# A graph network on one core: second layer moved ahead of the gathered rows' turning, results used a round later, eight slots in place of four

## Chip, cores and metric

One Trainium2 chip, one of its cores. The metric is the device time of one execution in microseconds, as the median of several runs; lower is better. The profile is one further execution of the same program.

## What is computed

A table of 12,500 nodes with 16 features and a list of 400,000 edges, sorted by receiver (`dst`), with 8 features each. Cut to what matters:

```
h = relu(layernorm(x));  x = x + degree-normed sum over edges of h[src] at dst
h = relu(layernorm(x))
n = LN(MLP(h));  e = LN(MLP(edge_attr))              # encoders, width 64
for s in 0, 1:
    e = e + LN(MLP_s(concat[e, n[src], n[dst]]))      # edge step
    agg = segment_sum(e, dst)
    n = n + LN(MLP'_s(concat[n, agg]))                # node step
out = x + decoder(n)
```

An MLP is `silu(a @ w0 + b0) @ w1 + b1`, all widths 64.

## The kernel before

Everything is float32 but for some helper products. Edges are worked through in 391 rounds of 1,024 slots. A round is two chunks of 512 edges, stacked on the 128 partitions (64 features each), and each chunk's receivers lie in one window of 64 nodes. After a preparation (lists, degrees) three stages run over all rounds, each an own block of programs for the engines:

- **the first layer** (`first_layer`, names `fl_`): the first sum over edges and the edge encoder. Sender rows of x are gathered by GpSimd into a ring of 64 rounds (`gather_sender_x`, L157), up to 53 rounds ahead of their use;
- **two edge steps** (`edge_step`, names `edge_blk_`). In each round GpSimd gathers 8 x 128 rows of the sender table (`sender_part`, L2053) into one of four buffers `g`, as soon as `pre` of four rounds back is signalled. SyncE loads the receivers' numbers `dlb`, the two windows `win` and the edge state `e` (256 KB), in `operands`, two rounds after its own loop count, and stores the new edge state in `store`. VectorE makes the one-hot matrices `oha` (receivers, for taking rows out of the window) and `ohb` (for summing). TensorE adds three products in one bank `h_ps`: window by one-hot (L2102), edge state by weight (L2104), and the gathered rows turned by the identity (L2107); then signals `pre`. ScalarE applies silu (`h`), TensorE the second layer (`second`, L2088 and L2090, into `y_ps`), ScalarE and VectorE the norm (`scale`, `normed`, giving `t`), TensorE the window sums (`sums`, L2069) and, in the first of the two steps (`keep`), the turning of `t` (`turn`, L2078); VectorE adds the sums to `agg` (`add_sums`, L2195) and makes the new edge state `new` (`finish`, L2203).

The order on each engine is written out by hand in a `body(n)`, with work of earlier rounds as `n.back(k)`. Before, TensorE's body of an edge step is: sums and turn of round n-3, second layer of n-1, then the three products of round n, the last of which waits for the gathers. VectorE's: both one-hots of n, addition and finish of n-3, norm of n-1.

The node steps run inside the stages: `rounds_and_nodes` has a main loop, and a late loop of 12 passes with 16 rounds each, into which the pieces of one node tile (`NodeTiles`, lines 1140 to 1380) are set per pass. The 13th node tile is done whole at the end (`nodes_again`), and its stores must be out before the next stage's gathers start.

`rounds_and_nodes` is where the code's size comes from. `Slot(m, b)` stands for round `m * QUAD + b`. `QUAD` is the number of buffers that the code writes out, and so the number of rounds in one pass of the main loop: with 4, the loop `Fori(2, 49)` has 47 passes of four rounds, with eight rounds written out before it and three after it. Semaphores of transfers also go by `n.b`, one for each of the QUAD slots.

Of the kernel before, what the change touches and what calls it, by code (L numbers as in the profile page):

```python
# [14 lines left out]
P = 128  # L15
# [7 lines left out]
TILES = 4  # L23
# [19 lines left out]
QUAD = 4  # L43
# [54 lines left out]
class Slot:  # L98
# [16 lines left out]
    @property  # L115
    def half(self):
        return self.b % 2

# [1393 lines left out]
def first_layer(nc, idx_all, loc_all, gr, g_in, take_ok, key_d, x_parts, part_f, buf, attr_d, xg_d, edge_d, base_sb, agg, enc_w0, w_mid, b1_parts, one_bf, sum_g, ident, row_f, vecs, eps_c, count_sb, raw, s_at, work):  # L1512

    with ExitStack() as ctx:
# [11 lines left out]
        attr = many(QUAD, "attr", [P, 8, E_DIM])  # L1526
        gx = many(QUAD, "gx", [P, TILES, 2, D + XG])
        t = many(QUAD, "t", [P, TILES, 2, D])
        ohb = many(QUAD, "ohb", [P, 8, WIN])
        e = many(QUAD, "e", [P, CHUNK])  # L1530
# [7 lines left out]
        low_key = many(QUAD, "low_key", [P, P], F16)  # L1538
# [25 lines left out]
        with nc.Block() as block:  # L1564
            @block.sync
            def _(sp):
                def store(n):
                    if n.exists():
                        wait(sp, e_ok, n)
                        sp.dma_start(edge_d[bass.ds(n.n, 1)].rearrange("a p c -> (a p) c"), e[n.b][:, :]).then_inc(e_out[n.b], 16)  # L1570

                def body(n, i=None, j=None):
                    wait(sp, turned_in, n.back(4))
                    sp.dma_start(attr[n.b][:, :, :], attr_v[bass.ds(unsorted + n.n, 1)].rearrange("a p j c -> (a p) j c")).then_inc(attr_in[n.b], 16)
                    wait(sp, hot_ok, n.back(4))
                    sp.dma_start(low_key[n.b][:, :], key_v[bass.ds(n.n, 1), PER, :].broadcast_to([P, P])).then_inc(key_in[n.b], 16)
# [21 lines left out]
            def _(pe):  # L1598
# [22 lines left out]
                def turn_in(n):  # L1621
                    wait(pe, attr_ok, n.back(1))
                    landed(pe, attr_in, n)
                    held(pe, passed)
                    nc.tensor.transpose(at_ps[0:64, 0:P], attr[n.b][:, :, :].rearrange("p j c -> p (j c)"),
                                        ident[:, :]).then_inc(turned_in, 1)

                def sums(n):
# [6 lines left out]
                    for c in range(2):  # L1635
                        to = agg_ps[0:XROW + XG, WIN * c:WIN * c + WIN]
                        for i in range(TILES):
                            ins = nc.tensor.matmul(to, gx[n.b][:, i, c, :], ohb[n.b][:, c * TILES + i, :],  # L1638
                                                   start=i == 0, stop=i == TILES - 1)
# [13 lines left out]
                def turn(n):  # L1653
# [3 lines left out]
                    for i in range(TILES):  # L1657
                        ins = nc.tensor.transpose(t_ps[:, P * i:P * i + P], t[n.b][:, i, :, :].rearrange("p c d -> p (c d)"),
# [37 lines left out]
                last = rounds_and_nodes(pe, body, count_sb, 2)  # L1696
# [14 lines left out]
            def _(act):  # L1711
# [38 lines left out]
                last = rounds_and_nodes(act, body, count_sb, 2)  # L1750
# [12 lines left out]
            def _(dve):  # L1763
# [7 lines left out]
                def one_hots(n):  # L1771
                    if not n.exists():
                        return
                    v.tensor_tensor(ohb[n.b][:, :, :], keys[:, 0:WIN].rearrange("p (j w) -> p j w", j=1).broadcast_to([P, 8, WIN]),  # L1774
# [9 lines left out]
                def scaled(n):  # L1784
# [5 lines left out]
                    for to in (t[n.b][:, :, :, :], gx[n.b][:, :, :, 0:D]):  # L1790
# [4 lines left out]
                def take(n):  # L1795
# [4 lines left out]
                    v.tensor_copy(gx[n.b][:, :, :, D:D + X_DIM].rearrange("p i c d -> p (i c) d")[:, 0:PER, :],  # L1800
# [3 lines left out]
                def hot(n):  # L1804
# [4 lines left out]
                    for c in range(KEYS // P):  # L1809
                        ins = v.tensor_scalar(low_hot[n.half][:, P * c:P * c + P], low_key[n.b][:, :], part4[:, c:c + 1], None, ALU.is_equal)  # L1810
                    ins.then_inc(hot_ok, 1)

                def select(n):
# [7 lines left out]
                    v.tensor_reduce(gx[n.b][:, TILES - 1, 1, D:D + X_DIM], of_top[:, :, :].rearrange("p h d -> p d h"), AX_X,  # L1821
# [15 lines left out]
                def finish(n):  # L1837
# [4 lines left out]
                    v.tensor_scalar(e[n.b][:, :], t_ps[:, :], col("g"), col("beta"), ALU.mult, ALU.add).then_inc(e_ok, 1)  # L1842
# [79 lines left out]
                for b in range(QUAD):  # L1922
# [24 lines left out]
                last = rounds_and_nodes(dve, body, count_sb, 2)  # L1947
# [18 lines left out]
def edge_step(nc, idx_all, loc_all, local_d, edge_d, ps_d, pr_d, base_sb, agg, w_in, w_mid, b1_parts, one_bf, ident, row_f, part64,  # L1966
              vecs, eps_c, mlp, keep, count_sb, work):

    with ExitStack() as ctx:
# [13 lines left out]
        dlb = many(QUAD, "dlb", [P, CHUNK], BF16)  # L1983
        win = many(QUAD, "win", [P, P])
        g = many(QUAD, "g", [P, TILES, P])
        e = many(QUAD, "e", [P, CHUNK])
        new = many(QUAD, "new", [P, CHUNK])
        t = many(QUAD, "t", [P, TILES, 2, D])
        ohb = many(QUAD, "ohb", [P, 8, WIN])
        oha = many(2, "oha", [P, CHUNK])  # L1990
# [3 lines left out]
        idle = sb("idle", [P, 2])  # L1994
# [12 lines left out]
        with nc.Block() as block:  # L2007
            @block.sync
            def _(sp):
                def store(n):  # L2010
                    if keep and n.exists():
                        wait(sp, new_ok, n)
                        sp.dma_start(edge_d[bass.ds(n.n, 1)].rearrange("a p c -> (a p) c"), new[n.b][:, :]).then_inc(e_out[n.b], 16)

                def operands(n):
# [4 lines left out]
                    for c in range(2):  # L2020
                        q = slice(64 * c, 64 * c + 64)
                        sp.dma_start(dlb[n.b][q, :], local_v[bass.ds(n.n, 1), c, :].broadcast_to([64, CHUNK])).then_inc(dlb_in[n.b], 16)
                    for c in range(2):
                        q = slice(64 * c, 64 * c + 64)
                        sp.dma_start(win[n.b][q, q], pr_d[bass.ds(at[c], WIN), :]).then_inc(win_in[n.b], 16)
# [10 lines left out]
                for k in (2, 1):  # L2036
                    operands(last.back(k))
                    store(last.back(k + 4))
                for k in (4, 3, 2, 1):
                    store(last.back(k))  # L2040
                if keep:
                    for k in (4, 3, 2, 1):
# [4 lines left out]
            def _(pool):  # L2047
                def body(n):
                    if n >= QUAD:
                        pool.wait_ge(pre, n - QUAD + 1)  # L2050
                    for j in range(8):
                        c, i = j // TILES, j % TILES
                        pool.indirect_dma_start(  # L2053
                            out=g[n % QUAD][:, i, 64 * c:64 * c + 64], out_offset=None, in_=ps_d,
# [6 lines left out]
            def _(pe):  # L2061
                def sums(n):
# [4 lines left out]
                    for i in range(TILES):  # L2067
                        for c in range(2):
                            ins = nc.tensor.matmul(agg_ps[D * c:D * c + D, 0:WIN], t[n.b][:, i, c, :],  # L2069
                                                   ohb[n.b][:, TILES * c + i, :], start=i == 0, stop=i == TILES - 1)  # L2070
                    ins.then_inc(sum_ok, 1)

                def turn(n):
# [3 lines left out]
                    for i in range(TILES):  # L2077
                        ins = nc.tensor.transpose(t_ps[:, P * i:P * i + P], t[n.b][:, i, :, :].rearrange("p c d -> p (c d)"),  # L2078
# [15 lines left out]
                def body(n, i=None, j=None):  # L2094
# [5 lines left out]
                    landed(pe, win_in, n, 32)  # L2100
                    wait(pe, oha_ok, n)
                    nc.tensor.matmul(h_ps[n.half][:, :], win[n.b][:, :], oha[n.half][:, :], start=True, stop=False)  # L2102
                    landed(pe, e_in, n)
                    nc.tensor.matmul(h_ps[n.half][:, :], w_in[:, :], e[n.b][:, :], start=False, stop=False)  # L2104
                    landed(pe, g_in, n, 128)
                    for i in range(TILES):
                        ins = nc.tensor.matmul(h_ps[n.half][:, P * i:P * i + P], g[n.b][:, i, :], ident[:, :], start=False,  # L2107
# [3 lines left out]
                last = rounds_and_nodes(pe, body, count_sb, 2)  # L2111
                for k in (3, 2, 1):
                    sums(last.back(k))
                    turn(last.back(k))
                    if k == 3:
# [4 lines left out]
            def _(act):  # L2120
                def warm(func):
                    k = 0 if func == ACT.Silu else 1
# [10 lines left out]
                def silu(n, i=None, j=None):  # L2133
                    warm(ACT.Silu)
# [5 lines left out]
                    warm(ACT.Sqrt)  # L2140

                def body(n, i=None, j=None):
                    scale(n.back(1))
# [4 lines left out]
                    silu(n, i, j)  # L2148
                    if i is not None:
                        nodes.act_late_dma(act, i, j)  # L2150

                nodes.act_begin(act)
                last = rounds_and_nodes(act, body, count_sb, 2)
# [8 lines left out]
            def _(dve):  # L2162
                v = nc.vector

                def one_hots(n):
                    landed(dve, dlb_in, n, 32)
                    wait(dve, pre, n.back(2))
                    v.tensor_tensor(oha[n.half][:, :], dlb[n.b][:, :], keys[:, WIN:WIN + 1].broadcast_to([P, CHUNK]),  # L2168
                                    ALU.is_equal).then_inc(oha_ok, 1)
                    v.tensor_tensor(ohb[n.b][:, :, :], keys[:, 0:WIN].rearrange("p (j w) -> p j w", j=1).broadcast_to([P, 8, WIN]),  # L2170
# [3 lines left out]
                def normed(n):  # L2174
# [7 lines left out]
                    v.tensor_tensor(t[n.b][:, :, :, :].rearrange("p i c d -> p (i c) d"), y_ps[n.half][:, :].rearrange("p (k d) -> p k d", d=D),  # L2182
# [15 lines left out]
                def finish(n):  # L2198
# [3 lines left out]
                    landed(dve, e_out, n.back(4))  # L2202
                    v.scalar_tensor_tensor(new[n.b][:, :], t_ps[:, :], col("g"), e[n.b][:, :], ALU.mult, ALU.add).then_inc(new_ok, 1)  # L2203
# [9 lines left out]
                for b in range(QUAD):  # L2213
# [5 lines left out]
                last = rounds_and_nodes(dve, body, count_sb, 2)  # L2219
                add_sums(last.back(3))  # L2220
                finish(last.back(3))
                normed(last.back(1))
                for k in (2, 1):
# [26 lines left out]
```

## Time and profile before

| | |
|---|---|
| median of 3 runs | 11666.72 us (11663.32 to 11670.03) |
| profiled execution, first to last instruction | 11672.6 us |
| first layer, main loop, then late loop | about 719 to 2018, then to 3712 us |
| first edge step, first to last gather | 3769.4 to 7676.2 us |
| second edge step, first to last gather | 7722.6 to 11628.2 us |
| busy share: GpSimd, TensorE, VectorE, ScalarE | 73%, 70%, 53%, 46% |

PE is TensorE's matmuls and PEld its weight loads, DVE is VectorE, ACT is ScalarE, POOL is GpSimd, SP is SyncE; a q behind the name means the engine's instruction queue (register work, branches, issued transfers), which isn't counted as busy. In a row, the name before "<-" is written and those behind it are read. "Idle before" an instruction is put down to what ended it; "issue" means that the engine waited for nothing that the profile shows. Times of places are in us from the first instruction.

### The profile page before, as it was taken

What the parts mean: (1) busy time and instruction counts of PE and PEld (TensorE: products, weight loads), DVE (VectorE), ACT (ScalarE), POOL (GpSimd) and SP (SyncE); (2) the same over time, 40 slices, a digit from 0 to 9 for tenths busy, and PEclk for the clock granted to TensorE, in tenths of its full rate; (3) what the DMA queues carried; (4) which work ended last, traced back from release to release, by engine and by line L of the source; (5) the groups of instructions that cost most, each with busy time, mean ns of one, the idle gap of its engine ahead of it and who ended that gap; (6) DMA issues with size and microseconds to landing.
All of it is one profiled execution on the core that took longest, in us unless ns stands there. A gap on an engine that the chain in (4) does not pass through costs nothing. (4 is left out here: it accounts for less than half of the span.)

```text
span 11672.6 us, 199199 instructions
## 1 busy us (share of the span) xinstructions
PE 8130.9 (70%) x55867; PEld 6189.3 (53%) x55867; DVE 6224.5 (53%) x13945; ACT 5398.6 (46%) x8550; POOL 8560.3 (73%) x9018
## 2 busy tenths in 40 slices
PE   5778888888887666666666666666666666666666
PEld 4667777666665444444455545444444444444444
DVE  9988888777776444444444444433333333333333
ACT  0146666555554444444444444444444444444444
POOL 6777777777772777777777777767777777777776
PEclk8789999999998888888888888878888888888888
DMA  2322222222222333333344434432222223323332
GB/s 75 63 44 53 53 53 54 52 53 53 53 52 50 93 97 95 95 95 95 97 104 103 102 100 102 104 78 70 69 69 69 69 70 72 72 71 73 72 72 58
DMA packets 1363893, 866.26 MB, mean 74 GB/s; under 512 B 896223, under 2 KB 1049840, under 8 KB 1362557
## 3 DMA queue, kind: packets, MB, share of 16 engines
q1 hardware_dynamic: 960162, 583.07, 18.3%
q0 software_dynamic: 287776, 227.99, 12.1%
q10 hardware_dynamic: 115376, 49.25, 1.7%
q14 instruction: 432, 3.54, 0.1%
q8 instruction: 147, 2.41, 0.1%
HBM read 627.59 MB, written 247.78 MB: 75 GB/s over the span
## 5 line engine op out<-in xcount | busy, mean ns | idle before, releaser
L2053 POOL DMA_INDIRECT edge_blk_g<-sender_part,idx_all x6256 | 5909.0, 945 | 2157.3 <-issue 1905.3
L2107 PE MATMUL edge_blk_hps<-ident,edge_blk_g 128*128 128x128 f32 x6256 | 1214.8, 354 | 2724.2 <-DMA edge_blk_g<-sender_part,idx_all 2724.2
L157 POOL DMA_INDIRECT gather_ring<-sender_x,idx_all x2422 | 2291.4, 946 | 775.9 <-issue 771.4
L2107 PEld LDWEIGHTS edge_blk_hps<-ident,edge_blk_g 128*128 128x128 f32 x6256 | 1021.2, 247 | 3373.2 <-DMA edge_blk_g<-sender_part,idx_all 3371.9
L2195 DVE SCALAR_TENSOR_TENSOR agg<-edge_blk_aggps,vecs,agg 64x64 f32 x1564 | 442.6, 283 | 3198.3 <-PE edge_blk_aggps L2069 3034.3
L2123 ACT ACT_TABLE_LOAD x1564 | 2006.6, 1283 | 60.2 <-ACTq L1151 32.0
L2137 ACT ACTIVATE edge_blk_h<-edge_blk_hps,vecs 128x512 f32<-128x512 f32 x782 | 537.5, 687 | 2972.2 <-PE edge_blk_hps L2107 2962.5
L2090 PEld LDWEIGHTS edge_blk_yps<-w_edge_blk,edge_blk_h 128*128 128x128 f32 x6256 | 1141.7, 255 | 65.0
L2178 DVE TENSOR_REDUCE edge_blk_red<-edge_blk_sq 128x8 f32<-128x512 f32 x782 | 536.2, 686 | 1157.0 <-ACT edge_blk_sq L2129 1134.0
L2090 PE MATMUL edge_blk_yps<-w_edge_blk,edge_blk_h 128*128 128x128 f32 x6256 | 1100.0, 335 | 0.0
L1714 ACT ACT_TABLE_LOAD x782 | 1003.3, 1283 | 33.2 <-PEq L95 19.0
L1638 PE MATMUL fl_aggps<-fl_ohb,fl_gx 128*96 128x64 f32 x6256 | 666.7, 264 | 452.8 <-DVE fl_ohb L1774 451.0
L1649 PE MATMUL fl_xps<-sender_x_parts,n_was 128*128 128x400 bf16 x4692 | 910.5, 347 | 3.2 <-DVE fl_ohb L1774 3.2
L1638 PEld LDWEIGHTS fl_aggps<-fl_ohb,fl_gx 128*96 128x96 f32 x6256 | 612.8, 177 | 538.6 <-DVE fl_ohb L1774 430.4
L2102 PE MATMUL edge_blk_hps<-edge_blk_oha,edge_blk_win 128*128 128x512 f32 x1564 | 851.3, 627 | 27.9 <-DMA edge_blk_win<-receiver_part 14.4
L1720 ACT ACTIVATE fl_sq<-fl_yps 128x512 f32<-128x512 f32 x391 | 233.3, 597 | 1244.5 <-PE fl_yps L1607 1142.5
L2104 PE MATMUL edge_blk_hps<-edge_blk_e,ew 128*128 128x512 f32 x1564 | 802.0, 594 | 0.0
L2069 PE MATMUL edge_blk_aggps<-edge_blk_ohb,edge_blk_t 128*64 128x64 f32 x12512 | 766.2, 290 | 7.6 <-DVE agg L2195 7.6
L2129 ACT ACTIVATE edge_blk_sq<-edge_blk_yps 128x512 f32<-128x512 f32 x782 | 465.1, 595 | 621.8 <-PE edge_blk_yps L2090 596.6
L2069 PEld LDWEIGHTS edge_blk_aggps<-edge_blk_ohb,edge_blk_t 128*64 128x64 f32 x12512 | 629.9, 193 | 147.1 <-issue 106.1
L1649 PEld LDWEIGHTS fl_xps<-sender_x_parts,n_was 128*128 128x128 bf16 x4692 | 479.7, 102 | 324.0 <-issue 55.7
L2168 DVE TENSOR_TENSOR edge_blk_oha<-edge_blk_dlb,edge_blk_keys 128x512 f32<-128x512 bf16 x782 | 529.4, 677 | 76.7 <-issue 57.9
(284 smaller groups left out, 12163.1 us busy)
## 6 DMA issues: line engine op xcount, KB each, us to landing
edge_blk_e<-edge_state SPq DMA_DIRECT2D x782, 256.0 KB
edge_state<-fl_e SPq DMA_DIRECT2D x391, 256.0 KB
edge_blk_g<-sender_part,idx_all POOLq DMA_INDIRECT x6256
edge_blk_dlb<-local_dst SPq DMA_DIRECT2D x1564, 64.0 KB
edge_state<-edge_blk_new SPq DMA_DIRECT2D x391, 256.0 KB
gather_ring<-sender_x,idx_all POOLq DMA_INDIRECT x2422
edge_blk_win<-receiver_part SPq DMA_DIRECT2D x1564, 16.0 KB
fl_attr<-attr_slots SPq DMA_DIRECT2D x391, 32.0 KB
```

Source lines behind the costliest of these rows:

```text
L157: pool.indirect_dma_start(out=gr[:, n % RING, ring_place(j), :], out_offset=None, in_=table, in_offset=bass.IndirectOffsetOnAxis(ap=idx_al ...
L1638: ins = nc.tensor.matmul(to, gx[n.b][:, i, c, :], ohb[n.b][:, c * TILES + i, :], start=i == 0, stop=i == TILES - 1)
L1649: ins = nc.tensor.matmul(x_ps[:, 0:TOPS * X_DIM], low_hot[n.half][:, P * c:P * c + P], x_parts[:, k, c, :], start=c == 0 and k == 0, stop= ...
L1714: nc.scalar.activation(idle[:, k:k + 1], eps_c[:, :], func)
L2053: pool.indirect_dma_start(out=g[n % QUAD][:, i, 64 * c:64 * c + 64], out_offset=None, in_=ps_d, in_offset=bass.IndirectOffsetOnAxis(ap=idx ...
L2069: ins = nc.tensor.matmul(agg_ps[D * c:D * c + D, 0:WIN], t[n.b][:, i, c, :], ohb[n.b][:, TILES * c + i, :], start=i == 0, stop=i == TILES - 1)
L2090: ins = nc.tensor.matmul(y[:, P * i:P * i + P], h[n.half][:, P * i:P * i + P], w_mid[:, :], start=False, stop=i == TILES - 1)
L2102: nc.tensor.matmul(h_ps[n.half][:, :], win[n.b][:, :], oha[n.half][:, :], start=True, stop=False)
L2104: nc.tensor.matmul(h_ps[n.half][:, :], w_in[:, :], e[n.b][:, :], start=False, stop=False)
L2107: ins = nc.tensor.matmul(h_ps[n.half][:, P * i:P * i + P], g[n.b][:, i, :], ident[:, :], start=False, stop=i == TILES - 1)
L2123: nc.scalar.activation(idle[:, k:k + 1], eps_c[:, :], func)
L2137: nc.scalar.activation(h[n.half][:, :], h_ps[n.half][:, :], ACT.Silu, bias=col("b0")).then_inc(h_ok, 1)
```

## The change

- `QUAD` goes from 4 to 8, and a new constant `BUFS = 4` with a property `buf` takes its place for nearly all buffers, which stay four. So the main loops have eight rounds in a pass, and there are eight transfer semaphores of each kind; `rounds_and_nodes` is called with one written-out pass instead of two.
- In the edge steps `e` has eight buffers, `new` is gone (the new edge state is written over `e`), `oha` has four buffers instead of two.
- TensorE's body: the products of window and edge state of round n, the second layer of n-1, the gathered rows of n, then sums and turn of n-4.
- VectorE's body: `receivers` (oha) of n, addition of n-5, `ohb` of n-1, finish of n-5, norm of n-2. ScalarE's: silu of n first, then the norm's part of n-1.
- SyncE stores eight rounds back, and loads `e` once the store of eight rounds back has landed.

The diff, cut:

```diff
-QUAD = 4
+QUAD = 8
+BUFS = 4
...
+    @property
+    def buf(self):
+        return self.b % BUFS
...
# first layer: all buffers n.b -> n.buf, and on every engine
-                last = rounds_and_nodes(sp, body, count_sb, 2)
+                last = rounds_and_nodes(sp, body, count_sb)
...
# edge step
-        new = many(QUAD, "new", [P, CHUNK])
-        oha = many(2, "oha", [P, CHUNK])
+        oha = many(BUFS, "oha", [P, CHUNK])
...
                     if keep:
-                        wait(sp, new_ok, n.back(4))
+                        landed(sp, e_out, n.back(QUAD))
+                    else:
+                        wait(sp, pre, n.back(QUAD))
                     sp.dma_start(e[n.b][:, :], edge_d[bass.ds(n.n, 1)]...).then_inc(e_in[n.b], 16)

                 def body(n, i=None, j=None):
                     operands(n.back(2))
-                    store(n.back(6))
+                    store(n.back(8))
...
+                def first(n):
+                    landed(pe, win_in, n, 32)
+                    wait(pe, oha_ok, n)
+                    nc.tensor.matmul(h_ps[n.half][:, :], win[n.buf][:, :], oha[n.buf][:, :], start=True, stop=False)
+                    landed(pe, e_in, n)
+                    nc.tensor.matmul(h_ps[n.half][:, :], w_in[:, :], e[n.b][:, :], start=False, stop=False)
+                    second(n.back(1))
+                    landed(pe, g_in, n, 128)
+                    for i in range(TILES):
+                        ins = nc.tensor.matmul(h_ps[n.half][:, P * i:P * i + P], g[n.buf][:, i, :], ident[:, :], ...)
+                    ins.then_inc(pre, 1)
+
                 def body(n, i=None, j=None):
-                    sums(n.back(3))
-                    turn(n.back(3))
-                    second(n.back(1))
+                    first(n)
+                    sums(n.back(4))
+                    turn(n.back(4))
                     if i is not None:
                         nodes.pe_late(pe, i, j)
-                    (the three products of n)
...
                 def body(n, i=None, j=None):          # ScalarE
-                    scale(n.back(1))
+                    silu(n, i, j)
                     if i is not None:
                         ...
-                    silu(n, i, j)
+                    scale(n.back(1))
...
                 def body(n, i=None, j=None):          # VectorE
-                    one_hots(n)
-                    add_sums(n.back(3))
-                    finish(n.back(3))
-                    normed(n.back(1))
+                    receivers(n)
+                    add_sums(n.back(5))
+                    one_hots(n.back(1))
+                    finish(n.back(5))
+                    normed(n.back(2))
...
                 last = rounds_and_nodes(dve, body, count_sb)
+                add_sums(last.back(5))
+                one_hots(last.back(1))
+                finish(last.back(5))
+                normed(last.back(2))
+                add_sums(last.back(4))
+                finish(last.back(4))
                 normed(last.back(1))
-                for k in (2, 1):
+                for k in (3, 2, 1):
                     add_sums(last.back(k))
                     finish(last.back(k))
```

## Rows read from the trace of the kernel before

**Rows 1.** The page, part 1: busy us, share, instructions.
```profile
PE 8130.9 (70%) x55867; PEld 6189.3 (53%) x55867; DVE 6224.5 (53%) x13945; ACT 5398.6 (46%) x8550; POOL 8560.3 (73%) x9018
```

**Rows 2.** GpSimd's waits over the span: us in total, times, longest.
```profile
POOL edge_blk_g L2053 <- issue: 1905.3, 6254, 0.3
...
POOL edge_blk_g L2053 <- POOLq L95: 252.0, 2, 206.6
```

**Rows 3.** Gathers of the first edge step: ns min/median/max, first and last start.
```profile
L2053 POOL DMA_INDIRECT edge_blk_g<-sender_part,idx_all x3128: 940/945/1353, 3769.4 to 7676.2; - x196
```

**Rows 4.** Waits between 4500 and 7500 us, as in rows 2.
```profile
PEld edge_blk_hps L2107 <- DMA edge_blk_g<-sender_part,idx_all: 1234.6, 301, 6.7
```

**Rows 5.** Stretches (main loop; late loops): PE, PEld, DVE, ACT, POOL busy (x count).
```profile
1509.70:1792.10 282.40, 245.98 (x2001) 202.98 (x2000) 250.55 (x641) 173.49 (x280) 213.53 (x227) 1.00 0.29 53
2315.10:3569.40 1254.30, 1046.27 (x7659) 844.28 (x7659) 984.91 (x2493) 647.25 (x1062) 943.64 (x999) 0.92 0.28 52
...
10028.30:11468.10 1439.80, 926.07 (x5661) 657.30 (x5661) 524.66 (x1099) 673.19 (x1054) 1088.81 (x1153) 0.84 0.31 72
```

**Rows 6.** VectorE's waits in ten main passes, 1509.7 to 1792.1 us.
```profile
DVE agg L1835 <- PE fl_aggps L1638: 23.6, 40, 0.8
```

**Rows 7.** The first edge step's end: start, us, engine, instruction.
```profile
7680.60 2.08 PE L2107 MATMUL edge_blk_hps<-ident,edge_blk_g 128*128 128x128 f32 x8 [6.62 <-DMA edge_blk_g<-sender_part,idx_all]
...
7684.64 1.05 PE L2090 MATMUL edge_blk_yps<-w_edge_blk,edge_blk_h 128*128 128x128 f32 x8
...
7687.65 0.69 DVE L2182 TENSOR_TENSOR edge_blk_t<-edge_blk_yps,edge_blk_rs 128x512 f32<-128x512 f32 x1
7689.72 0.70 DVE L2195 SCALAR_TENSOR_TENSOR agg<-edge_blk_aggps,vecs,agg 64x64 f32 x2 [1.38 <-issue]
...
7690.57 0.73 PE L2069 MATMUL edge_blk_aggps<-edge_blk_ohb,edge_blk_t 128*64 128x64 f32 x16 [3.67 <-DVE agg L2195]
...
7691.89 0.70 DVE L2195 SCALAR_TENSOR_TENSOR agg<-edge_blk_aggps,vecs,agg 64x64 f32 x2 [0.68 <-PE edge_blk_aggps L2069]
```

**Rows 8.** VectorE's main-loop branches, first layer: ns, first and last start.
```profile
L171 DVEq COMPARE_BRANCH  x47: 50/56/86, 718.8 to 2018.1; - x47
...
L171 DVEq COMPARE_BRANCH  x1: 56/56/56, 1509.7 to 1509.7; - x1
```

**Rows 9.** VectorE in order of time, main loop and late loop.
```profile
1505.42 0.67 DVE L1774 TENSOR_TENSOR fl_ohb<-fl_aggps,loc_all 128x512 f32<-128x512 f32 x1
...
1510.21 0.68 DVE L1791 TENSOR_TENSOR fl_gx<-fl_yps,fl_rs 128x512 f32<-128x512 f32 x1
...
1512.41 0.67 DVE L1774 TENSOR_TENSOR fl_ohb<-fl_aggps,loc_all 128x512 f32<-128x512 f32 x1
...
3014.89 0.69 DVE L1365 COPY n_stage<-fl_nps 128x512 f32<-128x512 f32 x1 [0.43 <-PE fl_nps L1268]
3018.89 0.63 DVE L1817 SCALAR_TENSOR_TENSOR fl_of_top<-row_f,n_hd,fl_xps 128x400 f32<-128x400 f32 x1 [3.31 <-issue]
```

**Rows 10.** One late-loop branch of VectorE and the record after it.
```profile
L176 DVEq COMPARE_BRANCH  x1: 63/63/63, 3015.0 to 3015.0; - x1
L176 DVEq FUSED_REGOPS  x1: 198/198/198, 3018.5 to 3018.5; - x1
```

**Rows 11.** ScalarE's in the same loop: first and last starts.
```profile
L176 ACTq COMPARE_BRANCH  x9: 45/45/56, 2319.9 to 3436.5; - x9
L176 ACTq FUSED_REGOPS  x9: 128/128/128, 2320.1 to 3436.8; - x9
```

**Rows 12.** VectorE's waits by issue, late loops of first layer, second step.
```profile
DVE fl_of_top L1817 <- issue: 29.7, 9, 3.7
...
DVE edge_blk_oha L2168 <- issue: 22.6, 9, 2.6
```

**Rows 13.** Instruction transfers, main loop (1021.5:1999.5), late loop (2315:3569): packets, MB.
```profile
q14 instruction: 6, 0.05, 0.0%
...
q14 instruction: 74, 0.61, 0.2%
```

More of the change, by code:

```diff
@@ L1695, in _ @@
                 pe.wait_ge(prepared, 1)
-                last = rounds_and_nodes(pe, body, count_sb, 2)
+                last = rounds_and_nodes(pe, body, count_sb)
                 second(last.back(2))
@@ L1749, in _ @@
                 nodes.act_begin(act)
-                last = rounds_and_nodes(act, body, count_sb, 2)
+                last = rounds_and_nodes(act, body, count_sb)
                 square(last.back(2))
@@ L1921, in _ @@
                     step(v.memset(a[:, :], 0.0))
-                for b in range(QUAD):
+                for b in range(BUFS):
                     step(v.memset(gx[b][:, :, :, D + X_DIM:], 0.0))
@@ L1946, in _ @@
                 nodes.dve_begin(dve)
-                last = rounds_and_nodes(dve, body, count_sb, 2)
+                last = rounds_and_nodes(dve, body, count_sb)
                 for k in (2, 1):
@@ L1993, in edge_step @@
         red, sd, rs = (sb(k, [P, 8]) for k in ("red", "sd", "rs"))
-        idle = sb("idle", [P, 2])
+        idle = sb("idle", [P, 2 * QUAD])
         h_ps = [ps(f"hps{i}") for i in range(2)]
@@ L2037, in _ @@
                     operands(last.back(k))
-                    store(last.back(k + 4))
-                for k in (4, 3, 2, 1):
+                    store(last.back(k + 6))
+                for k in (6, 5, 4, 3, 2, 1):
                     store(last.back(k))
                 if keep:
-                    for k in (4, 3, 2, 1):
+                    for k in range(QUAD, 0, -1):
                         landed(sp, e_out, last.back(k))
@@ L2048, in body @@
                 def body(n):
-                    if n >= QUAD:
-                        pool.wait_ge(pre, n - QUAD + 1)
+                    if n >= BUFS:
+                        pool.wait_ge(pre, n - BUFS + 1)
                     for j in range(8):
@@ L2092, in second @@
                     ins.then_inc(y_ok, 1)
+                def first(n):
[7 more added lines that the diff above has]
+                    for i in range(TILES):
+                        ins = nc.tensor.matmul(h_ps[n.half][:, P * i:P * i + P], g[n.buf][:, i, :], ident[:, :], start=False,
+                                               stop=i == TILES - 1)
+                    ins.then_inc(pre, 1)
                 def body(n, i=None, j=None):
-                    sums(n.back(3))
-                    turn(n.back(3))
-                    second(n.back(1))
+                    first(n)
+                    sums(n.back(4))
+                    turn(n.back(4))
                     if i is not None:
                         nodes.pe_late(pe, i, j)
[L2100 to L2107, printed above, removed]
-                                               stop=i == TILES - 1)
-                    ins.then_inc(pre, 1)
-                last = rounds_and_nodes(pe, body, count_sb, 2)
-                for k in (3, 2, 1):
+                last = rounds_and_nodes(pe, body, count_sb)
+                for k in (4, 3, 2, 1):
                     sums(last.back(k))
                     turn(last.back(k))
-                    if k == 3:
+                    if k == 4:
                         second(last.back(1))
@@ L2163, in _, with receivers @@
                 v = nc.vector
-                def one_hots(n):
[L2166 to L2170, printed above, removed]
+                def receivers(n):
+                    landed(dve, dlb_in, n, 32)
+                    wait(dve, pre, n.back(4))
+                    v.tensor_tensor(oha[n.buf][:, :], dlb[n.buf][:, :], keys[:, WIN:WIN + 1].broadcast_to([P, CHUNK]),
+                                    ALU.is_equal).then_inc(oha_ok, 1)
+                def one_hots(n):
+                    if not n.exists():
+                        return
+                    v.tensor_tensor(ohb[n.buf][:, :, :], keys[:, 0:WIN].rearrange("p (j w) -> p j w", j=1).broadcast_to([P, 8, WIN]),
                                     loc_all[:, bass.ds(n.n * 8, 8)].rearrange("p (j w) -> p j w", w=1).broadcast_to([P, 8, WIN]),
@@ L2218, in _ @@
                 nodes.dve_begin(dve)
-                last = rounds_and_nodes(dve, body, count_sb, 2)
-                add_sums(last.back(3))
-                finish(last.back(3))
+                last = rounds_and_nodes(dve, body, count_sb)
+                add_sums(last.back(5))
[4 more added lines that the diff above has]
+                finish(last.back(4))
                 normed(last.back(1))
-                for k in (2, 1):
+                for k in (3, 2, 1):
                     add_sums(last.back(k))
```

78 lines of the change are left out of this document (38 added, 40 removed).

## Prediction

> **What bounds the kernel now.** I read the page first. GpSimd has the most busy time [rows 1]; an average says little here, so I asked what it waits for. Its list is short [rows 2]: the 6,256 gathers of the two edge steps are preceded by "issue" (0.30 us each, its own pace), and only twice, for 252.0 us together, does it wait for a barrier. One edge step's 3,128 gathers start from 3769.4 to 7676.2 [rows 3]: 3906.8 / 3127 = 1.249 us each, 9.99 us for the eight of a round, without a gap. TensorE meanwhile waits for the landing of the gathers, 1234.6 us in 301 rounds [rows 4], 4.1 us a round. So both edge steps run at GpSimd's pace, and TensorE, VectorE and ScalarE have room in every round.
>
> The first layer is different. GpSimd is through with the ring gathers 206.6 us before its first edge gather (the longest wait of [rows 2]), at 3769.4 - 206.6 = 3562.8. In the main loop VectorE is busy 250.55 of 282.40 us [rows 5], and most of what it is idle is the wait for the window sums, 23.6 us in 40 rounds [rows 6], a round trip VectorE starts itself. There the order of work on VectorE sets the round. A microsecond lost by VectorE in the first layer moves the start of the edge steps, and so the end, by a microsecond.
>
> **The order change in the edge steps.** Each instruction of `second`, `sums`, `turn`, `silu`, `scale`, `receivers` and `one_hots` remains, once per round. Moving `second(n-1)` ahead of the gathers' landing lets TensorE do it inside the 4.1 us wait; the wait for the gathers only gets shorter. Value: 0 in steady state, since 9.99 us of GpSimd cover it. Without this cover the gain would be at most the 4.1 us per round that TensorE waits. Results are used a round later, so four receivers' one-hots instead of two are held, and stores go out two rounds later; `new` is gone and `e` has eight buffers. The load of `e` now waits for a store eight rounds back, over 70 us old. GpSimd waits for `pre` four rounds back as before, and that is three rounds ahead of need. Queued behind the new waits on SyncE are the loads of a round two ahead; they were two rounds early and stay so. So 0 for the 782 edge rounds; what would break it is rival 2.
>
> **The ends of the edge steps.** After the last gather nothing hides latency. Before [rows 7]: gathers used at 7680.60, `second` at 7684.64, `t` at 7687.65, an addition at 7689.72, the last sums at 7690.57, the last addition at 7691.89, and then the last node tile. After, TensorE has one more round's sums and turn ahead of `second` (with the additions between them about 2 us), and one more round of additions follows the last `t`: the step from addition to addition is 2.2 us (7689.72 to 7691.89). Finishing one more round's state costs VectorE some tenths. I take +5 us for the first step, +4 us for the second, which has no turning: +9, bounds +3 and +15.
>
> **The loops.** `QUAD` is also the unroll factor of `rounds_and_nodes`. The rounds are the same 391 per stage, but the main loop goes from 47 passes of four rounds to 23 of eight. On the first layer's VectorE a pass takes (2018.1 - 718.8) / 46 = 28.25 us [rows 8]; a round inside one takes 6.99 us (1505.42 to 1512.41, [rows 9]), so the return costs 28.25 - 4 x 6.99 = 0.28 us. Before: 46 x 0.28 = 12.9 us.
>
> What does a return cost when the body has eight rounds? The late loops, with 16 rounds in a pass, show that size matters. On VectorE in the first layer the late branch is at 3015.0 and its next record at 3018.5 [rows 10]; ScalarE in the same loop goes on after 0.2 us (2319.9 to 2320.1, [rows 11]). The time is paid as VectorE idle before its next operation: 29.7 us at 9 returns, and in the second edge step 22.6 us at 9 [rows 12]. Beside it stand instruction transfers: in 978 us of main loop 6 packets on q14 (GpSimd's own straight code), in nine passes of the late loop 74 of 0.61 MB, so 8 per pass of 8.2 KB [rows 13]. A body that is too long is fetched again in each pass, and the engine stands while its top arrives.
>
> How long is too long? I counted every record of an engine between two of its branches, register, wait and load records too (the views' counts leave these out). VectorE: 149 in a main pass of the first layer, 612, 377 and 345 in the late ones: the first goes on at once, the other three stall. SyncE: 377 and 413 stall, 154 doesn't. ScalarE: 168 to 179 don't. TensorE: 1,825 stalls, 1,454 doesn't. By operations alone the new pass has 128 (641 in ten passes, doubled), the late pass of the second edge step 1099 / 9 = 122 and stalls [rows 5]. In records it is 2 x 149 less the second loop control, about 290: between 179 and 345, so the trace doesn't decide it by size. It does by place. The times of the transfers fit a grid of 128 records per packet, each block fetched when the one before it is entered. On this grid the late bodies that stall touch four blocks, those that don't at most three. The main loop starts some 95 records into a block; the earlier `scale` waits for eight semaphores instead of four and adds about 6. 101 + 290 = 391, past 384, the end of the third block: it touches a fourth, by 7 records. I take it that VectorE stalls in each return. SyncE (88), ScalarE (78) and TensorE (866) stay below sizes that don't stall. In the edge steps' main loops VectorE has 186 and SyncE up to 220 records; a stall there of some 3 us per 80 us would lie under GpSimd.
>
> Price: 22 returns. The idle time in the late loop is 29.7 / 9 = 3.3 us; at that branch VectorE had 0.6 us of work left (to 3015.58), in the main loop it has 1.2 (from 1509.7 to 1510.89) [rows 8, 9], so 2.7 us. Low: 22.6 / 9 = 2.5 less half a microsecond, 2.0. High: 2.7 plus another 2, if the fourth block's transfer, which starts just before the return, is still in the way. Sum: 22 x 2.7 - 12.9 = +46.5 us, bounds +31 and +91. The ring gathers aren't in the way (GpSimd is 206.6 us ahead), so nothing hides it.
>
> The Trainium skill (Runtime: NRT & Kernel Launch, "Instruction fetch mechanics") gives an instruction memory of 512 instructions for most engines. By it the new body would fit and this sum be 22 x 0.28 - 12.9 = -6.7 us. The trace speaks against reading it as a loop that may be 512 long, since bodies of 345 and 377 records stall; its remark that a taken branch outside the current window forces a fetch is what rows 10 show.
>
> **Sum.** +46.5 (loops) + 9 (ends) + 0 (rounds) = +55.5 us. On the profiled execution (11672.6 us) that is 11728; on the median of the runs, 11666.72, it is 11722.
>
> **The rivals.**
> 1. No stall: the eight-round body stays in VectorE's instruction memory. By my grid it is 7 records from doing so, and no body between 179 and 345 records has been seen. 22 x 0.28 - 12.9 + 9 = +2 us: 11669, no measurable change. This is the one on the other side; what decides is whether the loop ends before the third block does. Chance 0.16. (The 512 instructions of the Trainium skill's page on the runtime, above, would give this case.)
> 2. Node tiles in the edge steps' late rounds hold VectorE and TensorE so long that GpSimd waits for `pre`. For it: TensorE now does the node work at the end of a round and next wants a one-hot that VectorE makes after its own node work. Against it: GpSimd has three rounds, some 25 us, before it waits, and none of its 6,254 issue gaps is over 0.3 us [rows 2]. Price 2 us for each of 24 tiles: +48, with the stall 11770. Chance 0.05.
> 3. The order change pays: a shorter edge round. It needs GpSimd to issue faster than 1.249 us; nothing in the change touches that, and TensorE's wait shows the room is unused already. 0.1 us for each of 782 rounds would be -78, with the stall 11644. Chance 0.03.
>
> **How the numbers follow.** My forecast has 0.76. Its own range: 22 x 2.0 - 12.9 + 3 = +34 to 91 + 15 = +106, so 11701 to 11773. The range to hold 8 in 10 reaches down to the no-stall case and gives up the top of the forecast's own range, which needs both high bounds: 11664 to 11765. A change within 0.2%, 23 us, can't be told from none in this kernel. Slower: 0.76 + 0.05 and less 0.01 for small stalls = 0.80; same: 0.16; faster: 0.04.
>
> **What would show it.** Right: VectorE idle for 2 to 3 us by "issue" before `select` (the L1817 of before) once per eight rounds in the first layer's main loop; q14 packets in it up from 6 by about four or five per pass of 57 us; GpSimd's barrier wait after the ring gathers longer by some 46 us; gathers of the edge steps still 1.249 us apart; 5 us more between the last gather of a step and what follows. Wrong: few q14 packets in the main loop (rival 1), gaps between GpSimd's edge gathers (rival 2), or less than 3,907 us from first to last gather of a step (rival 3).

## The result, and the profile after

The changed kernel takes 11775.31 us (median of 4 runs, 11770.53 to 11778.12), the kernel before, measured beside it, 11666.53 (11663.32 to 11670.03). The ratio is 1.0094, 95% interval 1.0079 to 1.0108: 108.8 us slower, about twice the 55.5 us forecast and above the range, which ended at 11765. The profiled execution has a span of 11773.7 us, for 11672.6 before.

GpSimd's waits (line, what it waited for; us in total, times, longest):

```profile
POOL edge_blk_g L2059 <- issue: 1906.1, 6254, 0.3
POOL gather_ring L162 <- issue: 867.4, 2724, 37.4
POOL edge_blk_g L2059 <- POOLq L96: 351.9, 2, 299.9
```

Against [rows 2] the gathers' own pace is the same to 0.8 us in 1,906, and the barrier wait between the ring gathers and the first edge gather grew from 206.6 to 299.9 us. So the first edge gather starts 91.6 us later (3861.0 for 3769.4), and nothing was lost inside the edge steps: the first one's gathers

```profile
L2059 POOL DMA_INDIRECT edge_blk_g<-sender_part,idx_all x3128: 940/944/1341, 3861.0 to 7765.3; - x196
```

are (7765.3 - 3861.0) / 3127 = 1.249 us apart, as in [rows 3].

VectorE's waits in the same stretch of the main loop as in [rows 13], 1021.5 to 1999.5 us, the windows of that stretch and of one return of the loop (columns as in [rows 5], PEclk being TensorE's granted clock), the instruction transfers of the stretch, and the branches of the loop:

```profile
DVE agg L1840 <- PE fl_aggps L1643: 89.4, 128, 1.9
DVE fl_of_top L1822 <- issue: 41.2, 16, 2.9
DVE fl_of_top L1822 <- PE fl_xps L1654: 18.6, 16, 1.2
```
```profile
1021.50:1999.50 978.00, 833.42 (x6373) 679.54 (x6373) 801.01 (x2039) 554.44 (x893) 739.33 (x784) 0.94 0.27 50
1180.00:1184.00 4.00, 1.99 (x13) 2.02 (x13) 2.98 (x9) 1.93 (x4) 3.08 (x4) 0.70 0.07 8
1184.00:1188.00 4.00, 4.00 (x17) 2.59 (x17) 2.80 (x7) 0.00 (x0) 2.99 (x4) 0.50 0.21 52
1188.00:1192.00 4.00, 3.62 (x27) 2.90 (x26) 2.81 (x9) 1.60 (x2) 2.87 (x4) 0.94 0.34 45
```
```profile
q14 instruction: 86, 0.70, 0.2%
```
```profile
L176 DVEq COMPARE_BRANCH  x23: 61/69/86, 746.3 to 2097.3; - x23
```

A pass takes (2097.3 - 746.3) / 22 = 61.41 us for eight rounds. Two passes before took 56.5 [rows 8]. The forecast stall is there, once per pass: `select` (L1822, VectorE's operation that reads `fl_xps`) comes 41.2 / 16 = 2.58 us late by "issue", and q14 carries 86 packets instead of 6. But that is only half of what a pass lost. The timeline of one return, VectorE and then TensorE:

```profile
1176.21 0.68 DVE L1796 TENSOR_TENSOR fl_gx<-fl_yps,fl_rs 128x512 f32<-128x512 f32 x1
1179.50 0.63 DVE L1822 SCALAR_TENSOR_TENSOR fl_of_top<-row_f,n_hd,fl_xps 128x400 f32<-128x400 f32 x1 [2.60 <-issue]
...
1181.10 0.67 DVE L1779 TENSOR_TENSOR fl_ohb<-fl_aggps,loc_all 128x512 f32<-128x512 f32 x1
...
1184.94 0.28 DVE L1840 SCALAR_TENSOR_TENSOR agg<-fl_aggps,sum_g,agg 96x64 f32 x1 [1.93 <-PE fl_aggps L1643]
...
1189.27 0.63 DVE L1822 SCALAR_TENSOR_TENSOR fl_of_top<-row_f,n_hd,fl_xps 128x400 f32<-128x400 f32 x1 [1.16 <-PE fl_xps L1654]
```
```profile
1172.15 1.57 PE L1643 MATMUL fl_aggps<-fl_ohb,fl_gx 128*96 128x64 f32 x16 [0.84 <-DVE fl_ohb L1779]
...
1174.01 2.19 PE L1654 MATMUL fl_xps<-sender_x_parts,n_was 128*128 128x400 bf16 x12
...
1182.01 2.79 PE L1643 MATMUL fl_aggps<-fl_ohb,fl_gx 128*96 128x64 f32 x16 [3.69 <-DVE fl_ohb L1779]
1184.59 1.06 PE L1663 MATMUL fl_tps<-ident,fl_t 128*128 128x128 f32 x4
1185.45 3.68 PE L1654 MATMUL fl_xps<-sender_x_parts,n_was 128*128 128x400 bf16 x12
```

While VectorE stands, TensorE runs out of work: it is idle 3.69 us ahead of the window sums, where 0.84 is usual. Behind this idle time the granted clock is 0.50 in the window from 1184 on, the lower of its two levels (1.2 GHz). The sums take 2.79 us instead of 1.57 and the twelve products of `look` (L1654, which make `fl_xps`) 3.68 instead of 2.19, and VectorE waits for both (1.93 us, usually 0.53, and 1.16 us, usually none). Over the 22 returns the interval from one-hot (L1779) to one-hot averages 9.66 and 9.76 us in the two rounds behind the return and 7.00 in the six others. A return that isn't fetched makes the second of the two 7.15 us (seen below, with 28 memsets). That is 2.7 us for the stall and 2.6 us for the slow clock after it. In the trace's record of the granted clock, the main loop has 22 stretches at 0.50, one for each return.

The tally, profile against profile, from the one-hots and the gathers: the main loop (one-hot of round 7 to that of round 199) 1356.0 to 1463.3 us, +107.3; the late loop (to the last one-hot) 1663.2 to 1648.5, -14.7; from the last gather of the first step to the first of the second 46.4 to 53.0, +6.6; behind the last gather of all 44.4 to 50.7, +6.3. Their sum is +105.5. The spans differ by 101.1: the two stretches of gathers are 2.5 and 0.8 us shorter, and 1.0 us is missing ahead of them. The profiled execution of the kernel before is longer than each of its timed runs (11672.6 us against 11663.32 to 11670.03), and that of the changed kernel isn't (11773.7), so the profiles show a few us less than the 108.8 us between the medians.

### The profile page after: what moved, and what is told of

Same layout as the page of the kernel before. It is cut to its first block and busy times, and to the rows that moved or that the text cites. A ratio compares the mean times of both kernels' runs of the same rounds, so it can differ in the third digit from the quotient of the medians.

```text
span 11773.7 us, 196982 instructions
## 1 busy us (share of the span) xinstructions
PE 8245.8 (70%) x55867; PEld 6134.1 (52%) x55867; DVE 6237.5 (53%) x13945; ACT 5328.8 (45%) x8550; POOL 8554.8 (73%) x9018
## 5 line engine op out<-in xcount | busy, mean ns | idle before, releaser
L2103 PE MATMUL edge_blk_hps<-edge_blk_oha,edge_blk_win 128*128 128x512 f32 x1564 | 1168.1, 838 | 278.5 <-DVE edge_blk_oha L2176 273.8
L2096 PEld LDWEIGHTS edge_blk_yps<-w_edge_blk,edge_blk_h 128*128 128x128 f32 x6256 | 859.8, 199 | 315.7 <-issue 290.1
L1654 PE MATMUL fl_xps<-sender_x_parts,n_was 128*128 128x400 bf16 x4692 | 940.1, 354 | 3.2 <-DVE fl_ohb L1779 3.2
L2105 PE MATMUL edge_blk_hps<-edge_blk_e,ew 128*128 128x512 f32 x1564 | 925.3, 677 | 0.0
L2096 PE MATMUL edge_blk_yps<-w_edge_blk,edge_blk_h 128*128 128x128 f32 x6256 | 853.5, 281 | 0.0
L2140 ACT ACTIVATE edge_blk_sd<-edge_blk_red,eps_c 128x8 f32<-128x8 f32 x782 | 234.9, 300 | 989.7 <-DVE edge_blk_red L2190 965.6
L2105 PEld LDWEIGHTS edge_blk_hps<-edge_blk_e,ew 128*128 128x128 f32 x1564 | 383.8, 245 | 560.8 <-issue 559.0
L1654 PEld LDWEIGHTS fl_xps<-sender_x_parts,n_was 128*128 128x128 bf16 x4692 | 490.6, 105 | 344.8 <-issue 87.6
```

What stands on the lines that cost most here:

```text
L1654: ins = nc.tensor.matmul(x_ps[:, 0:TOPS * X_DIM], low_hot[n.half][:, P * c:P * c + P], x_parts[:, k, c, :], start=c == 0 and k == 0, stop= ...
L2096: ins = nc.tensor.matmul(y[:, P * i:P * i + P], h[n.half][:, P * i:P * i + P], w_mid[:, :], start=False, stop=i == TILES - 1)
L2103: nc.tensor.matmul(h_ps[n.half][:, :], win[n.buf][:, :], oha[n.buf][:, :], start=True, stop=False)
```

## The experiments

**Moving the body in instruction memory.** The edit puts k one-column memsets on VectorE ahead of the first layer. They write a tile that nobody reads, once:

```diff
+        shift = sb("shift", [P, 28])
...
                 v.memset(zero_col[:, :], 0.0).then_inc(zero_ok, 1)
+                for k in range(28):
+                    v.memset(shift[:, k:k + 1], 0.0)
```

With 16 of them:

> The changed kernel with 16 more tiny memsets in VectorE's program, in the preparation where VectorE is waiting. Theory (place): on the grid of 128 records the first layer's main loop on VectorE then runs from 118 to 407, still four blocks, so it is fetched again in each return: 11775 us like the changed kernel, within 8. Rival (size): a body of 289 records stalls wherever it lies: 11775 too. Rival (any other layout helps): about 11660. This run is the control for the next one.

Measured: 11773.58 us (11771.51 to 11779.01), ratio to before 1.0095 [1.0078, 1.0112]. (The kernel before took 11663.53 us beside the runs with 16 and 28 memsets, `busy_pe` and `loops_alone`, and 11666.50 beside the other four.) The stretch has 87 q14 packets.

With 28:

> The same with 28 memsets, 12 more than the control. Theory (place): the loop then starts 2 records into a block and ends at 291, three blocks. No stall: the main loop takes 22 x 0.3 us for its returns instead of 22 x 5.4, so 112 us less than the changed kernel: 11663, between 11655 and 11672. Instruction packets of the main loop fall to GpSimd's. Rival (size): 11775, as before.

Measured: 11660.85 us (11649.75 to 11669.84), ratio 0.9998 [0.9988, 1.0008]. Twelve more memsets take 113 us away. The same stretch of the main loop, window and instruction transfers, and the branches:

```profile
1021.50:1999.50 978.00, 857.15 (x6965) 706.80 (x6965) 873.54 (x2232) 604.68 (x977) 739.65 (x783) 1.00 0.29 53
```
```profile
q14 instruction: 7, 0.06, 0.0%
```
```profile
L176 DVEq COMPARE_BRANCH  x23: 50/56/86, 746.4 to 1981.5; - x23
```

The clock is 1.00, the transfers are gone, and a pass takes 56.14 us. Operations, waits and order are those of the changed kernel; only the body's place differs. So each return of the changed kernel costs 61.41 - 56.14 = 5.27 us more than a return that isn't fetched.

**The edge of the block, from the other side.** The same edit with 112 and with 124 memsets:

> The changed kernel with 112 memsets. By the grid the main body (289 records) starts 86 records into a block and ends at 375, inside the third block by 9. Theory of blocks: no stall, main loop about 1347 us as with 28 memsets, clock 1.00; the late body of the first layer spans six blocks (116 + 607 = 723). Time: 11661 if the late loop doesn't care, 11676 if six blocks cost it 15 us. Rival: 28 records helped by another thing than the number of blocks (how far ahead of the branch the last boundary lies, for example): main loop about 1463 us, 11775.

> The changed kernel with 124 memsets, 12 more than the one beside it. The main body starts at 98 and ends at 387, three records inside the fourth block. Theory of blocks: it stalls like the changed kernel itself, main loop 1463 us, clock down to 0.5 behind each stall, some 86 packets on q14 in the window, 11775. Rival: three records in a fourth block cost nothing, or the grid's origin is off by more than two records: 11661.

Measured: 11668.97 us (11660.62 to 11679.6) with 112, 1.0002 [0.9993, 1.0011]; 11785.23 (11780.02 to 11787.02) with 124, 1.0101 [1.0085, 1.0116]. The main loop takes 1350.6 and 1452.5 us, the late loop 1661.1 and 1667.9. Again twelve memsets decide, in the other direction: with 112 nine q14 packets in the stretch and a clock of 1.00, with 124

```profile
1021.50:1999.50 978.00, 833.99 (x6442) 681.08 (x6441) 810.57 (x2061) 560.95 (x903) 739.54 (x783) 0.95 0.27 51
```
```profile
q14 instruction: 87, 0.71, 0.2%
```

By the grid, give or take a record or two, the body reaches 23 records into a fourth block with 16 memsets and 3 with 124; with 28 it lies in three, and with 112 it ends 9 records short of the fourth. So 28 memsets didn't help by a place of their own, since 112 do too. The four runs leave one other reading open: that what counts is how few records lie between the last boundary and the branch (3 to 23 where the body is fetched again, 35 and 119 where it isn't). The late loops speak against it: by the same count the changed kernel's late body of the second edge step ends some 58 records behind a boundary, the late body of the first layer some 99, and both stall.

**Keeping TensorE at work.** In the changed kernel, TensorE multiplies 28 times into the node tile's bank in each pass, at the round where the stall falls; nobody reads the result, and one wait was added ahead of the loop, until VectorE has read what the bank held:

```diff
+                    if n.b == 0 and i is None and not isinstance(n.m, int):
+                        for _ in range(28):
+                            nc.tensor.matmul(n_ps[:, 0:2 * P], one_bf[:, :], b1_parts[:, 0:2 * P], start=True, stop=True)
...
+                        if n.n == 7:
+                            pe.wait_ge(rows_read, 1)
```

> The changed kernel, and in the first round after each return of the first layer's main loop TensorE does 28 products more (96x256, bf16, about 3 us, results unused) while it would wait for VectorE. VectorE's stall of 2.6 us per return stays. Theory (clock): the second half of the loss, 2.7 us per return, is TensorE's granted clock at 0.50 after the idle time; with work in between it stays at 1.00, the sums take 1.57 us again instead of 2.79, and the time falls by 22 x 2.7 = 59 us to 11716 (11705 to 11735; part of it lost if 3 us don't cover the wait). Rival (the second half is a second fetch or VectorE's own order): 11775 or more, since the products come on top.

Measured: 11731.78 us (11729.98 to 11735.96), 1.0058 [1.0041, 1.0075], 43.5 us less than the changed kernel. VectorE's waits and the window of the stretch, and the round behind the stall on TensorE:

```profile
DVE agg L1846 <- PE fl_aggps L1644: 77.5, 132, 1.1
DVE fl_of_top L1828 <- issue: 43.7, 17, 2.6
```
```profile
1021.50:1999.50 978.00, 864.66 (x7078) 715.30 (x7079) 829.45 (x2117) 577.19 (x929) 739.62 (x783) 1.00 0.28 52
```
```profile
1167.53 3.22 PE L1674 MATMUL fl_nps<-b_parts,one_bf 96*128 96x256 bf16 x28
1171.33 1.54 PE L1644 MATMUL fl_aggps<-fl_ohb,fl_gx 128*96 128x64 f32 x16 [0.58 <-DVE fl_ohb L1785]
...
1173.15 2.19 PE L1655 MATMUL fl_xps<-sender_x_parts,n_was 128*128 128x400 bf16 x12
```

The stall stays (43.7 / 17 = 2.57 us) and the clock stays up: sums 1.54 us, `look` 2.19. The two long rounds are now 9.66 and 7.51 us, and the main loop has no stretch at the lower clock. The second half of the price was the clock. A pass takes 59.1 us, so a return still costs 3.0: 2.7 for the stall and 0.4 left in the second round, whose cause I didn't trace. The extra work costs 4.6 us once at the start (the one-hot of round 7 at 704.6 for 700.0) and 1.8 us in the last pass. These and the 0.4 us of each return make up most of the 15.5 us by which the saving falls short of 59.

**The loops without the new order.** The kernel before with eight rounds in a pass and the old edge steps:

```diff
-QUAD = 4
+QUAD = 8
+BUFS = 4
...
-                last = rounds_and_nodes(dve, body, count_sb, 2)
+                last = rounds_and_nodes(dve, body, count_sb)
```

> The kernel before with QUAD = 8 and BUFS = 4 alone: loops of eight rounds, but the old order in the edge steps, the new edge state in its own four buffers. Theory: the whole loss of the first layer is there (91.6 us at the start of the edge steps in the profile), the ends of the edge steps are as before (46.4 and 44.4 us after the last gather instead of 53.0 and 50.7): 13 us less than the changed kernel, 11762 (11752 to 11770). Rival (the order change costs the time): near 11667. Rival (the order change saves time in the steady rounds): over 11775.

Measured: 11760.58 us (11760.29 to 11761.83), 1.0083 [1.0066, 1.01]. The main loop takes 1463.2 us, as after the whole change; behind the two steps' last gathers it is 46.5 and 44.8 us, as before. The new order thus costs 14.7 us between the medians, 12.4 of them seen in these two places, and gives nothing back.

**The loops, moved.** The same kernel with the 28 memsets:

> The eight-round loops alone, with the old order in the edge steps, and 28 one-column memsets on VectorE ahead of the first layer (they write a tile nobody reads). My theory: the loss of the loops is all in the first layer's main loop, because its body touches a fourth block of 128 records. With 28 records more it lies in three. So 11760.58 less what 28 memsets took away from the changed kernel (11773.58 - 11660.85 = 112.7): 11648, which is 0.16% faster than before, since the ends of the edge steps are those of before. In the profile: some 1347 us for the main loop's rounds (round 7 to 199), about 7 packets on q14 in it, and 46 and 44 us behind the last gathers of the two edge steps. Rival: the ends are set by the loop length too and cost their 13 us here: 11661.

Measured: 11645.57 us (11636.62 to 11655.11, 11 runs), 0.9982 [0.9973, 0.9991]: the fastest of all, and faster than before by a little less than the 0.2% that I took as the limit of what can be told, though its interval ends below 1. The changed kernel with 28 memsets is 15.3 us slower (11660.85), which prices the new order a second time, less exactly: the kernel before differs by 3.0 us between the two measurements.

**Where the late loop's 14.7 us come from.** The kernel before with 32 memsets, which leave its main loop alone:

> The kernel before with 32 one-column memsets on VectorE. Its main loops keep their number of blocks. Its late loop of the first layer (612 records on VectorE) goes from six blocks (712 = 100 + 612 records, past 640) to five (4 + 612 = 616). This asks where the 14.7 us come from by which the changed kernel's late loop is shorter than before's (1648.5 for 1663.2 us). Theory: from the place of that body, five blocks for six: then the late loop takes about 1648 here too and the time is 11652. Rival: it comes from the loop control of eight rounds, or from how the fetches of several engines happen to meet: 11664 to 11670, the late loop about 1663.

Measured: 11650.15 us (11639.46 to 11659.03), 0.9988 [0.9979, 0.9997], 16.4 us less than before. Its late passes last (3689.4 - 2175.1) / 11 = 137.7 us, those of before 139.3, from the branches:

```profile
L176 DVEq COMPARE_BRANCH  x12: 55/63/74, 2175.3 to 3707.9; - x12
```
```profile
L176 DVEq COMPARE_BRANCH  x12: 55/63/74, 2175.1 to 3689.4; - x12
```

(first before, then with 32 memsets). So the gain in the late loop belongs to the place of VectorE's body too, not to eight rounds in a pass or to the new order. All profiles fit: the late loop takes 1663.2 and 1661.1 us in the two kernels whose body touches six blocks (before, and 112 memsets), and 1641.4 to 1649.0 us in the seven where I count five; 124 memsets are a case apart. Over the 11 late returns, before has 8.1 packets of q14 per pass, the one with 32 memsets 7.1, the changed kernel 7.1 (138.2 us a pass), the one with 112 memsets 8.1 (139.2 us). With 124 memsets I counted five blocks too, and yet it has 8.1 packets and 140.0 us; VectorE's waits from 2400 to 3500 us show why:

```profile
DVE fl_of_top L1825 <- issue: 43.5, 8, 6.0
```

Up to 6.0 us per return instead of the 3.3 of [rows 12]. By my count this body begins with the first record of a block. If the grid lies one record earlier than I put it, the body begins with the last record of a block, touches six, and two transfers must arrive one after the other before it can go on. That fits the packets, the 6.0 us, and also the main bodies above (that of 124 memsets then still reaches into the fourth block, by a record or two). It is argued from these counts; no run was made for it alone.

## Why the prediction was half right

- **Order change in steady state, 0:** held. Gathers 1.249 us apart, 0.3 us the longest issue gap in 6,254. Rivals 2 and 3 are out.
- **A body that touches a fourth block is fetched in each return, one of three isn't:** held, at both edges (28 and 112 memsets against 16 and 124). VectorE's main body has 289 records, 290 were forecast. The changed kernel's own edge steps agree: the late body of the first step has 357 records but three blocks, and its next record comes 0.3 us after the branch; that of the second has 341 in four, and its next record comes after 3.2 us. Rival 1, by which the body stays, was wrong by the few records that the prediction named. Behind it stood the Trainium skill (Runtime: NRT & Kernel Launch, "Instruction fetch mechanics") with 512 instructions of memory. The measurement decides: a 289-record loop was fetched again at each return. The two can be reconciled: with room for four blocks of 128, entering the fourth fetches the fifth, over the first. The trace with 16 memsets shows the fetches, a packet about 3.4 us ahead of the return, where the body enters its fourth block, and the next two 1.7 and 4.1 us behind it; what they overwrite is argued and not shown.
- **The price of a return, 2.7 us, up to 4.7:** this is the step that failed. It measured 5.49 us in the prediction's own terms (a pass less eight rounds), 5.27 us against a return that isn't fetched, both above the high bound. The idle time of VectorE itself was sized rightly, 2.58 us. I priced the return as that engine's idle time and stopped there. The upper bound's "another 2" was for a transfer in the way, and no such thing happened: with 16 memsets that transfer starts earlier, and VectorE idles as long (2.56 us for 2.58). What came instead is that the engine VectorE feeds goes idle too, its granted clock falls to half, and VectorE, whose round trip to TensorE sets the round [rows 6], waits for the slower sums and `look`. Holding the clock up took 43.5 of the 108.8 us away. The hint was in [rows 5]: the clock is 1.00 in the main loop and 0.92 in the late one, whose returns stall. The Trainium skill (TensorE: Matmul & The Clock Gate, "HAM oscillation — how this bites in real kernels") describes idle gaps inside a kernel that bring TensorE back to half clock. The trace agrees: 0.50 behind 3.69 us of idle time, 1.00 throughout where the idle time was filled.
- **The sum of the main loop:** with the measured pass, a return costs 61.41 - 8 x 6.99 = 5.49 us, and 22 x 5.49 - 12.9 = +107.9 us; +107.3 was measured.
- **Ends of the edge steps, +9:** +12.9 in the profile (6.6 and 6.3), 14.7 and 15.3 between medians. The first end, from the use of the last gathers: `second` follows after 6.5 us (4.0 in [rows 7]), `t` after 11.4 (7.1), the last addition after 18.0 (11.3).

```profile
7769.69 2.08 PE L2109 MATMUL edge_blk_hps<-ident,edge_blk_g 128*128 128x128 f32 x8 [5.17 <-DMA edge_blk_g<-sender_part,idx_all]
...
7776.22 1.05 PE L2096 MATMUL edge_blk_yps<-w_edge_blk,edge_blk_h 128*128 128x128 f32 x8
```
```profile
7777.31 0.60 ACT L2138 ACTIVATE edge_blk_sq<-edge_blk_yps 128x512 f32<-128x512 f32 x1 [0.93 <-PE edge_blk_yps L2096]
7778.44 0.70 DVE L2207 SCALAR_TENSOR_TENSOR agg<-edge_blk_aggps,vecs,agg 64x64 f32 x2 [1.11 <-issue]
...
7779.85 0.68 DVE L2190 TENSOR_REDUCE edge_blk_red<-edge_blk_sq 128x8 f32<-128x512 f32 x1
...
7781.13 0.69 DVE L2194 TENSOR_TENSOR edge_blk_t<-edge_blk_yps,edge_blk_rs 128x512 f32<-128x512 f32 x1
7782.94 0.70 DVE L2207 SCALAR_TENSOR_TENSOR agg<-edge_blk_aggps,vecs,agg 64x64 f32 x2 [1.12 <-issue]
...
7787.64 0.70 DVE L2207 SCALAR_TENSOR_TENSOR agg<-edge_blk_aggps,vecs,agg 64x64 f32 x2 [0.89 <-PE edge_blk_aggps L2075]
```

  The mechanism is the one forecast in kind. One more round's sums and turn ahead of `second` cost 2.5 us (2 forecast), and one more round of additions 2.3 (2.2). Between `second` and the last `t` the loss is 1.9 us, for which the prediction had "some tenths": the squares for the last norm are ready at 7777.91, but VectorE's order has one more addition and new edge state ahead of it, and they keep its reduction until 7779.85. The second step costs as much as the first, not 1 us less; I didn't look apart at which instruction makes that so.
- **The late loops, 0 by silence:** they gave 14.7 us back, because the added code moved VectorE's late body from six blocks to five. The prediction used the grid for one loop and not for the others. Carried through, it would have asked this question, though not known the size.

Signs in the trace that the prediction named: idle by "issue" before `select`, 2 to 3 us per eight rounds (2.58); four or five more q14 packets a pass (80 in 16 returns, 5.0); the barrier wait longer by 46 us (93); gathers 1.249 apart (yes); 5 us more behind a step (6.6 and 6.3).

## What to carry to other kernels

When a loop body grows, count the records of each engine, not the operations, and lay them on the grid of instruction blocks that the transfers show: whether the body fits goes by its first and last block, and a dozen instructions that have nothing to do with it, ahead of it in the engine's program, can be worth 1%. Do this for every loop behind an insertion, for those that shrink in blocks as well. And price a stall by following it once round: who feeds on the stalled engine, how long is that one idle, and does its clock fall.

## What the runs showed that I hadn't expected

- 12 one-column memsets outside of all loops change the time of 11,660 us by 113 us, down at one place and up, by 116 us, at another.
- A stall of 2.6 us on VectorE costs 5.3 us: TensorE's granted clock is 0.50 behind 3.69 us of idle time, and work of 1.57 and 2.19 us takes 2.79 and 3.68.
- 28 products whose result nobody reads, in each of 23 passes, made the kernel 43.5 us faster.
- The kernel before gains 16.4 us (0.12%) from 32 idle memsets, by one block fewer in its late loop.
